# Attention scores of two heads on the two halves of TensorE's rows: q and k in two fp32r parts of 62 rows instead of three bf16 parts of 108

## What is computed

```python
qkv = clip(einsum('bsd,ed->bse', hidden_states, Wqkv), -8, 8)
q, k, v = split(qkv, [512, 1024], axis=-1)
q = layer_norm(q, q_ln_w, q_ln_b)          # over all 512 columns
k = layer_norm(k, k_ln_w, k_ln_b)
q, k, v = (t.reshape(B, S, 32, 16) for t in (q, k, v))
scores = einsum('bqhd,bkhd->bhqk', q, k) * 16 ** -0.5
scores = scores + slopes[None, :, None, None] * (pos[None, :] - pos[:, None])
scores = where(causal, scores, -1e30)
probs = softmax(scores, axis=-1)
out = einsum('bhqk,bkhd->bqhd', probs, v).reshape(B, S, 512)
return einsum('bsd,ed->bse', out, Wout)
```

## Time and profile before

| | us |
|---|---|
| median of 3 timed runs (1145.27 to 1156.36) | 1147.9 |
| profiled execution, its own time | 1146.97 |
| its span | 1145.1 |
| PE busy in the span | 1077.1 (94%) |
| DVE busy | 876.7 (77%) |
| ACT busy | 663.8 (58%) |
| POOL busy | 368.6 (32%) |

### The profile page before, as it was taken

How to read it: one execution, slowest core, us unless ns; L and a number is a source line. 1 busy time by engine, 2 the same in 40 slices (tenths; PEclk the granted TensorE clock), 3 DMA queues, 4 the chain that set the end, 5 groups by cost and what they waited for, 6 DMA issues and landing times. The chain is left out here.

```text
span 1145.1 us, 18720 instructions
## 1 busy us (share of the span) xinstructions
PE 1077.1 (94%) x6401; PEld 676.6 (59%) x6401; DVE 876.7 (77%) x2083; ACT 663.8 (58%) x1061; POOL 368.6 (32%) x474
## 2 busy tenths in 40 slices
PE   5999988999999999999999998999999999999997
PEld 4788764433333333333333333788888888887885
DVE  6788897888887887888788782677867876777776
ACT  3666556666666676676767667544544454445443
POOL 2666635121211221121122112133424433343343
PEclk9999999999999999999999999999999999999999
DMA  6255753453445436343444512100110020012001
GB/s 209 77 154 154 200 131 124 123 134 87 114 105 155 106 93 143 84 133 83 144 107 118 125 51 87 37 1 10 58 45 1 19 93 1 1 37 74 1 1 38
DMA packets 99663, 98.95 MB, mean 86 GB/s; under 512 B 28144, under 2 KB 81008, under 8 KB 99568
## 3 DMA queue, kind: packets, MB, share of 16 engines
q1 hardware_dynamic: 97936, 97.36, 31.1%
q10 hardware_dynamic: 1632, 0.39, 0.2%
HBM read 76.09 MB, written 21.23 MB: 85 GB/s over the span
## 5 line engine op out<-in xcount | busy, mean ns | idle before, releaser
L893 ACT ACTIVATE pr<-pair 128x1024 f32<-128x1024 f32 (+3 forms) x384 | 293.2, 811 | 151.5 <-PE pair L1010 97.0
L268 DVE CUSTOM_DVE_ANT_0 bank<-bank,sg 128x384 f32<-128x384 f32 (+1 forms) x488 | 227.6, 522 | 65.7 <-PE bank L278 62.7
L1270 DVE SCALAR_TENSOR_TENSOR gate<-pair,sgu,gate 128x512 f32<-128x512 f32 x168 | 126.1, 751 | 94.9 <-PE pair L1349 94.9
L1348 PE MATMUL pair<-xc_lo,w_gu 128*128 128x512 f32 x448 | 175.6, 392 | 1.5 <-DVE xc_lo L1253 1.5
L1349 PE MATMUL pair<-xc_hi,w_gu 128*128 128x512 f32 x448 | 174.7, 390 | 0.0
L271 DVE TENSOR_REDUCE mx<-bank 128x1 f32<-128x512 f32 x240 | 150.2, 683 | 8.9 <-PE bank L278 8.2
L1140 POOL TENSOR_TENSOR h_lo<-gate,h_hi 128x512 fp32r<-128x512 f32 x56 | 72.5, 1294 | 241.8 <-ACT h_hi L1165 241.8
L1190 ACT ACTIVATE gate<-gate 128x512 f32<-128x512 f32 x56 | 35.5, 634 | 168.5 <-DVE gate L1270 168.5
L278 PE MATMUL bank<-ks,qs 108*128 108x512 bf16 (+3 forms) x384 | 107.7, 329 | 5.4 <-DVE mx L268 5.1
L278 PE MATMUL bank<-xin_c,s_sb 108*128 108x512 bf16 (+3 forms) x344 | 97.5, 332 | 4.6 <-DVE mx L268 4.3
L1005 PE MATMUL pair<-s_sb,xin_c 111*128 111x512 bf16 (+3 forms) x384 | 94.4, 330 | 7.8 <-ACT dt L396 2.9
(11 more groups left out here) (116 smaller groups left out, 1955.5 us busy)
## 6 DMA issues: line engine op xcount, KB each, us to landing
stk<-parts SPq DMA_DIRECT2D x16, 768.0 KB, 5.6
zst<-in_z_all SPq DMA_DIRECT2D x24, 448.0 KB, 4.2
xin_c<-in_x SPq DMA_DIRECT2D x32, 256.0 KB, 3.0
sst<-in_w_all SPq DMA_DIRECT2D x16, 448.0 KB, 6.0
s_sb<-stk SPq DMA_DIRECT2D x96, 64.0 KB
xin_c<-stk SPq DMA_DIRECT2D x96, 64.0 KB
qs<-stk SPq DMA_DIRECT2D x96, 64.0 KB
ks<-stk SPq DMA_DIRECT2D x96, 64.0 KB
```

The costliest lines, as they stand in the source:

```text
L268: dve.tensor_tensor_reduce(out=src, in0=src, in1=tri[:, 512 - w:512], scale=1.0, scalar=-3.0e38, op0=ALU.add, op1=ALU.max, accum_out=dst). ...
L893: act.activation(pr[e % 3][:, 2 * p:2 * p + 2, 0:w], pair[p][:, :, 0:w], ACT.Exp, scale=SCALE)\
L1270: dve.scalar_tensor_tensor(out=a, in0=GB[j % 4], scalar=scale_of(n, k, it), in1=a, op0=ALU.mult, op1=ALU.add)\
L1348: pe.matmul(GB[j % 4], w, xc_lo[:, k, :], start=True, stop=False)
```

## The change

Four things change. The parts of q and k become two fp32r parts, high and low, so a head has 3 x 16 + 12 = 62 rows, plus 2 for the maximum. Two heads share the 128 rows: head `2n` on rows 0 to 63, head `2n + 1` on rows 64 to 127, and each matmul of the scores names 62 or 64 rows of its half. The plan puts the pieces in pairs of two heads. The constant ALiBi rows have to be fp32 in DRAM, so GpSimd casts them in eight pieces in the first four tiles of stage A and SP stores them (`cast_row`, `store_row`). `residual` and `mid` go; `chain` has three operations instead of five; `send_d` issues two DMAs instead of one; a `load` of one half issues 16 DMAs instead of 14.

```diff
+PARTS = 3 * HD
+BIAS = 12
+ROWS_MAX = PARTS + BIAS
+ROWS = ROWS_MAX + 2
-    stk = nc.dram_tensor("stk", [2, BATCH, P, KT, 3, SEQ], BF16).ap()
+    stk = nc.dram_tensor("stk", [2, BATCH, P, KT, 2, SEQ], F32).ap()
+    q32 = nc.dram_tensor("q32", [GROUPS, BIAS, GH, SEQ], F32).ap()
+    k32 = nc.dram_tensor("k32", [GROUPS, BIAS + 3, GH, SEQ], F32).ap()
...
-            for r, both in enumerate(((0, 0), (1, 0), (2, 0), (0, 1), (1, 1), (0, 2))):
+            for h in range(2):
+                r0 = 64 * h
+                for r, both in enumerate(((0, 0), (0, 1), (1, 0))):
+                    rows = slice(r0 + r * HD, r0 + (r + 1) * HD)
+                    for a, dst in enumerate((qs[s][rows, b, :, :], ks[s][rows, :, cols])):
+                        src = stk[a, i // GROUPS, p0:p0 + 64, g // 2, both[a], cols]
+                        sp.dma_start(dst.bitcast(F32), src.rearrange("(n h c) s -> h c n s", n=2, h=2)[h]).then_inc(stk_in[s][b], 16)
...
-            total, work = sum(width[lo:hi]), sum(pc[3] + 60 for pc in lot)
+            total, work = sum(width[lo:hi]), sum(pc[3] + 110 for pc in lot)
...
-                    out[h].append(lot[at])
-                    at += 1
+                    out[h] += lot[at:at + 2]
+                    at += 2
...
-            pe.matmul(b[:, 0:w], qs[s][0:ROWS_MAX, qt // 4, j, (qt % 4) * P:(qt % 4 + 1) * P],
-                      ks[s][0:ROWS_MAX, j, k0:k0 + w], start=True, stop=True).then_inc(m_full, 1)
+            rows = slice(64 * (j % 2), 64 * (j % 2) + ROWS_MAX)
+            pe.matmul(b[:, 0:w], qs[s][rows, qt // 4, j // 2, (qt % 4) * P:(qt % 4 + 1) * P],
+                      ks[s][rows, j // 2, k0:k0 + w], start=True, stop=True).then_inc(m_full, 1)
...
+        def cast_row(pool, n):
+            rows = GROUPS * (BIAS + (3 if n >= GH else 0))
+            pool.wait_ge(row_in, 32)
+            if n > 0:
+                pool.wait_ge(row_out, 16 * n)
+            pool.tensor_copy(row32[0:rows, :], row16[n // GH][0:rows, n % GH, :]).then_inc(row_cast, 1)
+        def store_row(sp, n):
+            rows, dst = ((GROUPS * BIAS, q32), (GROUPS * (BIAS + 3), k32))[n // GH]
+            sp.wait_ge(row_cast, n + 1)
+            sp.dma_start(dst[:, :, n % GH, :].rearrange("g r s -> (g r) s"), row32[0:rows, :]).then_inc(row_out, 16)
...
-            act.dma_start(qs[s][ROWS_MAX:ROWS, b, :, :].rearrange("a j (t c) -> a (j t) c", c=P), dt_sb[b][:, :])\
-               .then_inc(done, 16)
+            for h in range(2):
+                dst = qs[s][64 * h + ROWS_MAX:64 * h + ROWS, b, :, :].rearrange("a n (t c) -> a (n t) c", c=P)
+                act.dma_start(dst.bitcast(F32), dt_sb[16 * h:16 * h + 16, :]).then_inc(done, 16)
...
                     if t < TILES - 2:
                         clip_v(pool, t)
+                    for n in row_parts(t):
+                        cast_row(pool, n)
...
-                    if t > 1:
-                        mid(t - 2, 1)
...
-                        if t > 1:
-                            residual(dve, t - 2, 1)
...
                     for jj in range(2):
-                        j = 2 * p + jj
-                        mm = pe.matmul(pair[p][:, jj, 0:512 - c0], ks[s][0:ROWS, j, kt * P:(kt + 1) * P],
-                                       qs[s][0:ROWS, qb, j, c0:512], start=True, stop=not diag[e])
+                        rows = slice(64 * jj, 64 * jj + ROWS)
+                        mm = pe.matmul(pair[p][:, jj, 0:512 - c0], ks[s][rows, p, kt * P:(kt + 1) * P],
+                                       qs[s][rows, qb, p, c0:512], start=True, stop=not diag[e])
```

More of the change, by code:

```diff
@@ L89, in build @@
         mx1 = sb("mx1", [P, 2, GH, 4], F32)
+        with ExitStack() as c0:
+            qs, ks = [sb_in(c0)("qs0", [P, 2, 2, 512], F32R)], [sb_in(c0)("ks0", [P, 2, SEQ], F32R)]
         s_sb = sb("s_sb", [P, 4, 512], F32)
@@ L137, in build @@
             sst = sbb("sst", [P, HALF], F32)
-            qs.append(sbb("qs1", [P, 2, GH, 512], BF16))
-            ks.append(sbb("ks1", [P, GH, SEQ], BF16))
+            with ExitStack() as c3:
+                row16 = [sb_in(c3)(f"row16{n}", [P, GH, SEQ], BF16) for n in range(2)]
+            qs.append(sbb("qs1", [P, 2, 2, 512], F32R))
+            ks.append(sbb("ks1", [P, 2, SEQ], F32R))
             vs.append(sbb("vs1", [P, QT, GH * VW], F32))
@@ L142, in build @@
             dneg = sbb("dneg", [P, 16], F32)
-            dres = sbb("dres", [P, 16], F32)
-            d3 = sbb("d3", [P, 3, 16], BF16)
-            dt_sb = [sbb(f"dt{n}", [48, P], BF16) for n in range(2)]
+            d2 = sbb("d2", [P, 2, 2, 2, 4], F32R)
+            dt_sb = sbb("dt", [32, P], F32)
             rec = sbb("rec", [P, 2, 4, GH], F32)
@@ L175, in load @@
             cols = slice(b * 512, (b + 1) * 512)
-            p0 = (i % 2) * 64
-            for r, both in enumerate(((0, 0), (1, 0), (2, 0), (0, 1), (1, 1), (0, 2))):
[L178 to L187, removed]
+            g, p0 = i % GROUPS, (i % 2) * 64
+            for h in range(2):
[5 more added lines that the diff above has]
+                        sp.dma_start(dst.bitcast(F32), src.rearrange("(n h c) s -> h c n s", n=2, h=2)[h]).then_inc(stk_in[s][b], 16)
+                sp.dma_start(qs[s][r0 + PARTS:r0 + ROWS_MAX, b, :, :].bitcast(F32),
+                             q32[g, :, :, cols].rearrange("r (n h) s -> h r n s", h=2)[h]).then_inc(stk_in[s][b], 16)
+                sp.dma_start(ks[s][r0 + PARTS:r0 + ROWS, :, cols].bitcast(F32),
+                             k32[g, 0:BIAS + 2, :, cols].rearrange("r (n h) s -> h r n s", h=2)[h]).then_inc(stk_in[s][b], 16)
             if b == 0 and values:
@@ L229, in spread @@
                 passed += width[h]
-                while at < len(lot) and (h == hi - 1 or sum(pc[3] + 60 for pc in lot[:at]) < work * passed / total):
-                    out[h].append(lot[at])
-                    at += 1
+                while at < len(lot) and (h == hi - 1 or sum(pc[3] + 110 for pc in lot[:at]) < work * passed / total):
+                    out[h] += lot[at:at + 2]
+                    at += 2
             return out
@@ L298, in build @@
         qk_var, qk_rstd, qk_ln = sem("qk_var"), sem("qk_rstd"), sem("qk_ln")
[L299 to L301 removed]
+        qk_ps, aff_done, part_h, part_l, part_out = (
+            sem("qk_ps"), sem("aff_done"), sem("part_h"), sem("part_l"), [sem(f"part_out{n}") for n in range(2)])
+        row_in, row_cast, row_out = sem("row_in"), sem("row_cast"), sem("row_out")
         mask_in = sem("mask_in")
@@ L422, in _ @@
                         sp.dma_start(behind[:, :], behind_in).then_inc(mask_in, 16)
+                    if 1 <= t <= 4:
+                        for n in row_parts(t - 1):
+                            store_row(sp, n)
                     if t == 6:
+                        sp.wait_ge(row_out, 16 * 2 * GH)
                         pairs_stored(sp, 2)
@@ L683, in _ @@
                 maxima(t, 3)
-                residual(dve, t - 1, 1)
                 maxima(t, 4)
@@ L966, in _ @@
                 dve.memset(b_o[:, :], 0.0).then_inc(o_clear, 1)
-                for a in range(2):
-                    residual(dve, TILES - 1, a)
                 def body(i, s, ip, last):
```

92 lines of the change are left out of this document (34 added, 58 removed).

## The result

The changed kernel takes 1316.7 us (median of 4 runs, 1307.4 to 1330.5) beside 1149.9 for the kernel before: 1.142 times as long, interval 1.131 to 1.153. The forecast was 1144, with a range up to 1200. The profiled execution spans 1319.9 us, 174.8 more than before.

What follows compares the result with a forecast made beforehand. TensorE was taken to bound stage B, with VectorE close behind and becoming the first stretch's bound. Against 1146.97 us, -6 over 16 groups and +3 in stage A gave 1144; range 1105 to 1200.

Steps and rivals of the forecast that it cites:

- The halves run together: Stage B scores: matmuls of two heads on separate row halves run at once, costing one stream or two weight loads.
- 0.22 us for a couple at every width, two loads at 0.11: Stage B scores: a pair of two heads costs two fp32r weight loads, against 0.43 us before at 512 columns.
- the 5.2 us of the first stretch: Stage B group, first score to end of step 8: TensorE saves 2.5 us in second pass, 2.7 in pieces.
- The switches, 0.22 the round trip: Stage B, between half-row and 128-row matmuls: 16 round trips a group, 2.2 us in first stretch, 1.3 in second.
- VectorE becomes the bound of the first stretch, 22.1 us: Stage B group through step 8: TensorE needs 19.9 us, VectorE 20.94 plus 1.2 idle, so 1.7 us less.
- Steps 9 to 11, 11.3 us: Second stretch of a stage B group: 10.0 us before plus 1.3 for switches.
- Stage A, +3 us: Stage A: casts and stores delay q's factor, counted as 5 us, less 2 us from 130 us on.
- The bound of 26 us: Stage A: upper bound for the delay by GpSimd's casts and store waits, 4 tiles at 6.5 us.
- The first (halves not together): Rival on stage B scores: row halves don't run together; a group takes 38.1 us, the kernel 1219; 18 in 100.
- The second, slower with a dear switch: Rival: halves run together, but fp32r loads lie bare after switches, round trip above 0.27 us; kernel 1163; 23 in 100.
- The third, faster: Rival: loads of the halves overlap and row switches are cheap; a group takes 30.5 us, the kernel 1097; 24 in 100.
- the last sign: Sign of being wrong: stage A ends over 8 us later than 192, adding its own cost to any case.

Runs made afterwards that it cites:

- e4: The kernel before with its score matmuls reading only 65 and 66 rows instead of 108 and 111, exp's scale smaller: 1238.7 and 1257.7 us.
- e2: The changed kernel with both heads of a pair on the same half of the rows, so no two run at once: 1390.2 and 1465.7 us.
- e7: e1 with each head's causal mask added by two matmuls of 64 rows instead of one of 128: 1219.9 us.
- e3: The kernel before with its score matmuls reading only 60 and 62 rows instead of 108 and 111, exp's scale smaller: 1273.3 and 1300.3 us.
- e8: e1 with each couple of matmuls of the second pass issued twice into the same banks: 1247.5 us, ratio 1.087.
- e9: e1 with both the mask on row halves (as in e7) and the second pass issued twice (as in e8): 1211.3 us.
- e1: The changed kernel with the ALiBi rows as fp32 constants copied within DRAM by two DMAs, no casts on GpSimd: 1279.8 us, ratio 1.113.
- e11: e9 with the pieces of the first pass planned one at a time instead of in twos: 1189.4 us.
- e12: e11 without the doubled second pass, that is e7 with its pieces one at a time: 1193.1 us.

## Why the prediction was wrong, point by point

**The missing term.** The prediction read 1.00 in the column of the clock in the earlier trace rows and took it for given in every case, rivals too. No step of its sum asks whether the change moves the clock. The change halves the rows that work in each matmul of the scores; e4 shows that this alone brings the granted clock of stage B to 0.80. Without it the kernel would stand near 1235 (1147 + 30.5 + 58), which is over the range too, so the terms below had failed as well. The Trainium skill (TensorE: Matmul & The Clock Gate, What's actually happening) says that the clock is set by how busy TensorE has been. By it a stage with TensorE busy for 94% before and 93% after would keep its clock; the measurement decides, and e4, 95% busy at 0.80, is against it.

**The halves run together:** right. Two matmuls of 0.39 us end within 0.39, and e2, where they don't, is 2.3 us a group longer.

**0.22 us for a couple at every width, two loads at 0.11:** the wrong mechanism, and a size that is right only for part of the couples. The two loads don't queue, they run together (0.19 us for both, above). Where a couple's loads ran under the couple ahead and no switch follows, it holds TensorE for 0.23 us at 512 columns and 0.18 at 384 (e7, 327.08 and 330.20). In the changed kernel the same couple has 0.32 before a mask, 0.28 at 384; the 0.09 more is the way into the switch, which the prediction priced apart. But a couple that stands behind a mask or a product with v loads its weights bare and holds TensorE for 0.34 at 512 columns (455.70, 459.05), where a pair took 0.43 before. In steps 4 to 8 that is every couple of 512-wide pieces: each was to save 0.21 us and saved 0.09, where VectorE didn't hold it up as well. This is the part of the 5.2 us of the first stretch that failed.

**The switches, 0.22 the round trip:** right, 0.20 by e3 against e4 and 0.21 by e7. 10 + 6 trips times 0.22 are 3.5 us a group; taking the mask's away saved 2.0, as a part went into waits: two pieces before a product take 0.66 us in e8 (255.45) and 0.87 in e9 (250.31), where the load of the second waits 0.28 us for VectorE.

**VectorE becomes the bound of the first stretch, 22.1 us:** wrong. 36.5 less the 9.85 of steps 9 to 11 is 26.6, in a group in which VectorE is busy for 26.8 of 38.2 (e8). VectorE waited for TensorE longer than TensorE and its loads for VectorE; of stage B from 230 to 780 us:

```profile
DVE bank L271 <- PE bank L282: 129.1, 77, 6.0
PE bank L282 <- DVE mx L271: 14.8, 44, 0.5
PEld bank L282 <- DVE mx L271: 61.1, 136, 1.7
```

Columns are the total, the times and the longest. The coupling that the prediction named ("the second of a pair finds VectorE one piece behind at most") is there, as the 0.90 us at 456.58, and was priced as idle time that stays. It costs both sides: TensorE stands for the second piece, and VectorE has nothing to do when TensorE then runs the second pass. Steps 4 to 8 at full clock take 14.74 us (455.06 to 469.80), where they took 12.71 before (433.28 to 445.99). The first row is where step 9 starts before, the second where it starts now:

```profile
445.99 0.50 PE L1005 MATMUL pair<-qs,ks 111*128 111x384 bf16 x2
```

```profile
469.80 0.44 PE L1004 MATMUL pair<-qs,ks 62*128 62x384 f32 x2
```

**Steps 9 to 11, 11.3 us:** too high, but by its base. They take 9.85 us (469.80 to 479.65). The 10.00 of the earlier trace rows starts at 445.53, 0.46 us ahead of step 9, and holds the wait of 0.76 us for the maxima, which is gone. From 445.99 to 455.53 without that wait are 8.78 us, so the steps grew by 1.07 where 1.3 was forecast: the reasoning held. For the same reason the base of 33.8 us a group was high; most groups took 32.6 to 32.9.

**Stage A, +3 us:** wrong, +30.5, of which 23 are the casts and stores. A cast took 1.04 us, less than the 1.9 of the sum. The stores between were mis-sized: 2.7 us to landing was the median of other stores. GpSimd, with its wait before each cast in brackets:

```profile
36.97 1.04 POOL L352 CAST row<-row 96x1024 f32<-96x1024 bf16 x1 [10.36 <-DMA q<-row]
...
80.66 1.04 POOL L352 CAST row<-row 120x1024 f32<-120x1024 bf16 x1 [10.04 <-DMA k<-row]
```

Up to 10.4 us; in the two tiles between it was 3.27 and 3.94. Ahead of the first of these stores SP had issued a store of v and four loads, among them a block of the weights, in 2.4 us. That the wait comes from these was not tested. The prediction had seen the path (q's factor, VectorE, then the transposes): TensorE waited for just that,

```profile
PE pair L727 <- DVE qk L631: 22.6, 6, 8.9
```

and was busy for 77 of the 100 us from 30 to 130, at a clock of 0.86 there. The bound of 26 us was near, the value taken from it was not. What the visits of pieces cost is read from e1, whose stage A is in step with before: 2.5 us more work for TensorE from 130 to 190 us (54.54 against 52.04) where 4 was forecast. No run shows the 7 us that the residuals were to free.

**The rivals.** The first (halves not together) has the wrong mechanism and came nearest with 1219. That was luck: it needs pairs without gain, and the couples run together. The second, slower with a dear switch, had the right sign; it wanted a round trip above 0.27 us, and that is 0.20. The third, faster, was right that the loads of the two halves run together; it is refuted by the switches, which are not cheap, and by the load that lies bare behind each. All three priced TensorE at a fixed clock.

**A slip of count:** the texts above the result have 62 rows plus 2 for the maximum. It is 3 x 16 + 12 = 60, and 62 with the two, as the shapes 60x512 and 62x512 show. No price hangs on it. "The bytes are the same" holds for the parts of q and k alone: the 12 ALiBi rows have twice the bytes, and stage B moves 62 MB instead of 58.6 (93 GB/s over 666.8 us, 112 over 523).

**The signs on record.** The two matmuls of a couple start together, and stage A ends over 8 us late, as the last sign warned. VectorE's share was to rise above 85% and is 62%; steps 9 to 11 were to be longer than 10 us and are 9.85.

## What to carry to other kernels

When a change makes matmuls use fewer rows, the clock is a term of the sum. One run of the old kernel with fewer rows read, nothing else changed, prices it before anything is rebuilt. Price a packed couple together with what stands before and behind it: beside other shapes each change costs about 0.1 us on either side, and one pass packed between unpacked work can give back all that packing saves. Handing an engine's partner its work in twos through three buffers costs both.

## What the runs showed of the hardware

- TensorE was granted 0.80 over a stage with 65 and 66 rows at work (e4) and 0.67 where fp32r matmuls of 60 and 62 rows never ran two at a time (e2), while it was busy for 95% of it; with 96 rows and more it was 1.00 in the profiled runs. The means are made of stretches at one level or the other: in the changed kernel 1.00 from 455 to 479 us and 0.50 from 490 to 530.
- Useless work can pay: a second pass issued twice brought 0.84 to 0.97 and took 32 us off the kernel (e8). Beside single pieces it was even in the sum (e11 1189.4, e12 1193.1 us, within their spread).
- Rows do as columns do: 62 rows between matmuls of 128 cost 0.20 us a round trip, 66 rows nothing.
- The fp32r weight loads of two row halves run together, two in 0.19 us, and so do the matmuls. Behind a matmul of another shape the loads lie bare: 0.34 us for a couple of 512 columns instead of 0.23.
- A single piece on one half starts together with a couple of the second pass, without being planned as a partner. In e12, both at the same moment by the record:

```profile
284.16 0.49 PE L283 MATMUL bank<-ks,qs 60*128 60x512 f32 x1
284.16 0.44 PE L1003 MATMUL pair<-qs,ks 62*128 62x384 f32 x1
```

- Left open: why the mask on halves raised the clock from 0.84 to 0.89 (e7), though its matmuls use half the rows; and what in a group decides that one runs at 1.00 and the next, with the same instructions, at 0.56 (e4).
